# VectorE's order within a group of the RWKV stage: residual, bonus product and moments change places

## The chip, the core and the metric

The kernel runs on one core of one Trainium2 chip. The metric is device time in microseconds, the median of several runs. It has five engines that run side by side and meet through semaphores: TensorE (PE; its weight loads are shown apart as PEld), VectorE (DVE), ScalarE (ACT), GpSimd (POOL) and SyncE (SP), which issues transfers here. Each takes its instructions in the order of its own program. On-chip memory is SBUF, and PSUM in banks, where PE writes.

## What is computed

The kernel is a chain of eight residual stages over x of shape 32 x 256 x 128 in float32. The change touches the first alone, an RWKV time mix behind a layernorm:

```python
shifted = jnp.pad(x, ((0, 0), (1, 0), (0, 0)))[:, :T]
delta = shifted - x
low = jnp.tanh((x + delta * mu_x) @ W_x1).reshape(B, T, 5, PROJ_LR)
mus = jnp.einsum('blnr,dnr->blnd', low, W_x2) + x_bias
xr, xw, xk, xv, xg = [x + delta * mus[:, :, i] for i in range(5)]
...
def step(S, inp):
    o_t = einsum('bhk,bhkv->bhv', r_t, S) + einsum('bhk,hk,bhk,bhv->bhv', r_t, u, k_t, v_t)
    S = exp(w_t)[..., None] * S + k_t[..., :, None] * v_t[..., None, :]
...
o = (o - mean) * rsqrt(var + EPS)          # per head
o = (o * gn_w + gn_b) * (g * sigmoid(g))
return o @ W_o                             # added to x
```

## The kernel before

`stage_rwkv` (from L282) works on 8192 tokens as 16 groups (NG) of 512 tokens, two sequences each. Its loop on every engine is a software pipeline written out by hand: one pass g holds work for group g-2 (end) up to group g+3 (start), and the order inside a pass is the order in which the engine does it. A step starts once the semaphores named in it are up.

VectorE's steps, by group p:

- `moments` (L359): mean and variance of the input rows, four bn_stats (L366) and seven small operations, the last of them vareps (L380).
- `mix_in` (L382): xm, the input of the low-rank projection. `mix_out` (L388), five times: xi from PE's mixes in PSUM.
- `outer` (L394), four times: kv, PE's value times key. The third value on PE waits for the first kv, the fourth for the second.
- `scan` (L401), four times two scans (L407) over 256 steps: the recurrence. Its inputs are dec and kv, both in SBUF.
- `bonus_key` (L410): ruk. `bonus_value` (L416): cv, PE's product c, in PSUM bank 3, times vv.
- `gate` (L422): gg from th (ScalarE) and PE's gate product.
- `variance` (L428) and `normalise` (L432): per-head norm, in n.
- `gated` (L450): z = nt * gg. `residual` (L456): PE's y, in PSUM bank 4, added to x.

GpSimd does `inverse` (L503): rstd and shift from vareps and the mean, `difference` (delta), three `add_x` (L519) and four `read` (L526) a pass. ScalarE's pass (L762) runs: square of group g-1, evac g+2, tw, vv, root (L691: logarithm and exponential of the norm), key, decay, gate (th, L735), receptance (rr), then `layernorm(g+3)` (four xn, L748, which wait for shift), then `affine(g-1)` (nt, L718), then the two low-rank tanh (L760). PE's pass (L658) runs: four values (L556), five mixes (L568), out g-2 (L633), heads g-1 (L643, L647), turn_in g+2 (L575, which writes bank 4 and waits for residual g-2), then decay_low, plain_value, key, decay, gate, bonus (L618), receptance, turn_back g-1 (L592), low_rank g+2 (L654, L656). The first low-rank product writes bank 3, so it waits for cv:

```python
def low_rank(p):
    pe.wait_ge(s["xm_done"], p + 1)
    at_least(pe, s["cv_done"], p - 1)
```

Of the kernel before, what the change touches and what calls it, by code (L numbers as in the profile page):

```python
# [84 lines left out]
def at_least(eng, sem, v):  # L85

    if not (isinstance(v, int) and v <= 0):
        eng.wait_ge(sem, v)
# [193 lines left out]
def stage_rwkv(nc, k, tag, w, x_in, arrive, loads):  # L282
# [5 lines left out]
    with ExitStack() as ctx:  # L288
# [54 lines left out]
        has = lambda p: 0 <= p < NG  # L343
# [8 lines left out]
        def _(dve):  # L352
# [29 lines left out]
            def mix_in(p):  # L382
                dve.wait_ge(s["delta_done"], p + 1)
                at_least(dve, s["low_done"], 2 * p)
                nc.vector.scalar_tensor_tensor(out=seq(xm[:]), in0=seq(delta[:, p % 2, :]), scalar=w["a_mux"][:, 0:1], in1=x(p),
                                               op0=ALU.mult, op1=ALU.add).then_inc(s["xm_done"], 1)

            def mix_out(p, j):  # L388
                i = ORDER[j]
                dve.wait_ge(s["mus_done"], 5 * p + j + 1)  # L390
                nc.vector.scalar_tensor_tensor(out=xi[:, i, :], in0=at[f"m{j}"], scalar=w["a_xb"][:, i:i + 1],
                                               in1=delta[:, p % 2, :], op0=ALU.add, op1=ALU.mult).then_inc(s["dm_done"], 1)

            def outer(p, v):  # L394
                dve.wait_ge(s["v_done"], VQ * p + v + 1)
                if v == 0:
                    dve.wait_ge(s["k_out"], p + 1)
                at_least(dve, s["scan_done"], VD * (p - 1) + 2 * v + 2)
                nc.vector.tensor_tensor(kv[:, v, :], vp[:, v % 2, :], kk[:, p % 2, :], ALU.mult).then_inc(s["kv_done"], 1)

            def scan(p, v):  # L401
                if v == 0:
                    dve.wait_ge(s["dec_done"], p + 1)
                dve.wait_ge(s["kv_done"], VQ * p + v + 1)
                at_least(dve, s["rs_done"], VQ * (p - 1) + v + 1)
                for b in range(2):
                    nc.vector.tensor_tensor_scan(S[:, v, b, 1:T + 1], dec[:, p % 2, b * T:(b + 1) * T], kv[:, v, b * T:(b + 1) * T], 0.0,  # L407
                                                 ALU.mult, ALU.add).then_inc(s["scan_done"], 1)

            def bonus_key(p):  # L410
                dve.wait_ge(s["r_out"], p + 1)
                at_least(dve, s["c_done"], p)
                nc.vector.scalar_tensor_tensor(out=ruk[:], in0=rr[0:HK, p % 2, :], scalar=w["a_u"][0:HK, 0:1], in1=kk[0:HK, p % 2, :],
                                               op0=ALU.mult, op1=ALU.mult).then_inc(s["ruk_done"], 1)

            def bonus_value(p):  # L416
                dve.wait_ge(s["c_done"], p + 1)
                dve.wait_ge(s["vv_out"], p + 1)
                at_least(dve, s["oc_done"], p)
                nc.vector.tensor_tensor(cv[:], at["c"], vv[:, p % 2, :], ALU.mult).then_inc(s["cv_done"], 1)  # L420

            def gate(p):  # L422
                dve.wait_ge(s["th_done"], p + 1)
                at_least(dve, s["z_done"], p - 2)
                nc.vector.scalar_tensor_tensor(out=gg[:, p % 3, :], in0=th[:], scalar=1.0, in1=at["gate"],
                                               op0=ALU.add, op1=ALU.mult).then_inc(s["gg_done"], 1)

            def variance(p):  # L428
                dve.wait_ge(s["sq_done"], p + 1)
                nc.vector.tensor_reduce(out=ss[:], in_=sq[:], axis=AX.X, op=ALU.add).then_inc(s["norm"], 1)  # L430

            def normalise(p):  # L432
                base = NORM * p
                dve.wait_ge(s["norm"], base + 1)
                nc.vector.tensor_scalar(ve[:], ss[:], 1.0 / VD, LN_EPS, ALU.mult, ALU.add).then_inc(s["norm"], 1)
                dve.wait_ge(s["y0_done"], p + 1)
                dve.wait_ge(s["norm"], base + 2)
                nc.vector.tensor_tensor(nw[:, 0, :], ve[:], y0[:], ALU.mult).then_inc(s["norm"], 1)
                dve.wait_ge(s["norm"], base + 3)
                nc.vector.scalar_tensor_tensor(out=nw[:, 1, :], in0=nw[:, 0, :], scalar=-0.5, in1=y0[:],  # L440
                                               op0=ALU.mult, op1=ALU.mult).then_inc(s["norm"], 1)
                dve.wait_ge(s["norm"], base + 4)
                nc.vector.scalar_tensor_tensor(out=nw[:, 2, :], in0=nw[:, 1, :], scalar=1.5, in1=y0[:],
                                               op0=ALU.add, op1=ALU.mult).then_inc(s["norm"], 1)
                dve.wait_ge(s["norm"], base + 5)
                at_least(dve, s["nT_done"], p)
                nc.vector.tensor_tensor(heads_of(n[:]), heads_of(oc[:]), nw[:, 2, :][:, :, None].to_broadcast([P, GT * HA, VD]),
                                        ALU.mult).then_inc(s["n_done"], 1)

            def gated(p):  # L450
                dve.wait_ge(s["nt_out"], p + 1)
                dve.wait_ge(s["gg_done"], p + 1)
                at_least(dve, s["y_done"], p)
                nc.vector.tensor_tensor(z[:], nt[:], gg[:, p % 3, :], ALU.mult).then_inc(s["z_done"], 1)

            def residual(p):  # L456
                dve.wait_ge(s["y_done"], p + 1)
                xg = k.X[:, p * GT:(p + 1) * GT, :].rearrange("p a b -> p (a b)")
                nc.vector.tensor_tensor(xg, at["y"], xg, ALU.add).then_inc(s["res_done"], 1)

            for g in range(-3, NG + 2):
                if has(g - 2):
                    gated(g - 2)
                if has(g):
                    for v in range(VQ):
                        outer(g, v)
                if has(g + 1):
                    mix_out(g + 1, 0)
                    mix_out(g + 1, 1)
                if has(g):  # L470
                    scan(g, 0)
                    bonus_key(g)
                if has(g + 1):
                    mix_out(g + 1, 2)
                    mix_out(g + 1, 3)
                    mix_out(g + 1, 4)
                if has(g):
                    scan(g, 1)
                if has(g - 2):
                    residual(g - 2)  # L480
                if has(g):
                    scan(g, 2)
                    scan(g, 3)
                if has(g - 1):
                    variance(g - 1)
                if has(g + 2):
                    mix_in(g + 2)
                if has(g - 1):
                    normalise(g - 1)
                if has(g + 3):  # L490
                    moments(g + 3)
                if has(g + 1):
                    gate(g + 1)
                if has(g):
                    bonus_value(g)
            dve.wait_ge(s["res_done"], NG)

        @block.gpsimd
# [2293 lines left out]
```

## Time and profile before

| | |
|---|---|
| Time, median of 3 runs | 3493.65 us (3492.93 to 3501.08) |
| The profiled execution | 3497.12 us, its span 3495.3 us |
| RWKV stage | from 16.2 to about 490 us of the span |
| PE busy over the whole span | 3058.7 us (88%) |
| DVE | 2353.5 us (67%) |
| ACT | 1738.7 us (50%) |
| POOL | 1241.1 us (36%) |
| VectorE's 128 scans in this stage, mean | 1163 ns |

The rows are read so. A timeline row gives start, length, engine, line, operation, what is written and read, the number of instructions merged, and in brackets how long the engine stood idle before it and who ended that. A windows row gives a stretch, its length, the busy time of each engine in it, and the granted TensorE clock (PEclk, 1.00 being full) in that stretch. On VectorE the next instruction starts up to 0.08 us before the profile has the one before it end.

### The profile page before, as it was taken

The numbers are of one execution on the slowest core, as the hardware profiler recorded it, in microseconds if no ns is written. First come the engines' busy times: TensorE is split into PE (matmuls) and PEld (weight loads), VectorE is DVE, ScalarE is ACT, GpSimd is POOL, SyncE is SP. The second block draws the span as 40 slices with busy tenths as digits, with TensorE's granted clock in tenths as the row PEclk, the third lists the DMA queues.
The fourth block names the chain that finished last, engine by engine and source line by source line (L and its number), as shares of the span: only waits on it lengthen the run. The fifth ranks groups of instructions, "written<-read, shape, count | busy, mean of one in ns | idle before, by whom it ended". The sixth has DMA issues, their size and how long they took to land. (4 is left out here: it accounts for less than half of the span.)

```text
span 3495.3 us, 49585 instructions
## 1 busy us (share of the span) xinstructions
PE 3058.7 (88%) x16500; PEld 2031.7 (58%) x16500; DVE 2353.5 (67%) x5412; ACT 1738.7 (50%) x3804; POOL 1241.1 (36%) x1238
## 2 busy tenths in 40 slices
PE   6999974999883799999649998889799999999989
PEld 2555554888741344444548887679645555555557
DVE  4888876555465677776655555213489999999964
ACT  2444321333352699999313333225366666666644
POOL 3444431000023477777310000422134444444432
PEclk9999976999997799999769999559999999999999
DMA  3000012111032101000221100000000000000001
GB/s 113 1 1 1 1 31 76 37 37 35 1 104 92 41 26 30 28 27 16 83 71 37 37 29 27 0 0 1 1 1 1 1 1 1 1 1 1 1 13 37
DMA packets 106556, 91.30 MB, mean 26 GB/s; under 512 B 15373, under 2 KB 96147, under 8 KB 104000
## 3 DMA queue, kind: packets, MB, share of 16 engines
q1 hardware_dynamic: 104928, 87.31, 7.9%
q8 instruction: 135, 2.21, 0.3%
q14 instruction: 117, 0.96, 0.1%
q10 hardware_dynamic: 1376, 0.82, 0.1%
HBM read 57.66 MB, written 30.15 MB: 25 GB/s over the span
## 5 line engine op out<-in xcount | busy, mean ns | idle before, releaser
L2370 ACT ACTIVATE m_x_hT<-m_x_hid,wm_b 128x260 f32<-128x260 f32 x512 | 242.8, 478 | 437.1 <-PE m_x_hid L2292 437.1
L1319 POOL TENSOR_TENSOR c_tE<-c_tE,c_tDm 128x256 f32<-128x256 f32 x512 | 373.4, 730 | 138.8 <-ACT c_tE L1279 125.4
L1202 DVE TENSOR_REDUCE c_tM<-c_tpa 128x2 f32<-128x512 f32 x512 | 330.2, 682 | 131.3 <-PE c_tpa L1104 130.4
L1279 ACT ACTIVATE c_tE<-c_tpb 128x512 f32<-128x512 f32 x512 | 310.0, 607 | 43.2 <-PE c_tpb L1121 43.2
L2292 PE MATMUL m_x_hid<-m_x_xg,wm_w 128*128 128x260 f32 x1024 | 306.7, 386 | 8.8 <-ACT m_x_hT L2370 5.3
L2300 PE MATMUL m_x_yp<-m_x_hT,wm_w 128*128 128x260 f32 x1024 | 301.1, 384 | 0.0
L1655 POOL TENSOR_TENSOR b_wkv<-b_at,b_rec 128x512 f32<-128x512 f32 x128 | 163.3, 1276 | 305.9 <-DVE b_rec L1591 305.9
L2148 POOL TENSOR_TENSOR rstd_all<-m_x_vareps,m_x_neg_half 128x8 f32<-128x8 f32 x16 | 26.4, 1649 | 654.0 <-DVE m_x_vareps L2231 654.0
L1104 PE MATMUL c_tpa<-c_tK,c_Qm 96*128 96x256 f16 x1024 | 205.3, 283 | 49.8 <-DMA c_Qm<-aug_d 36.6
L1121 PE MATMUL c_tpb<-c_Qm,c_tK 101*128 101x256 f16 x1024 | 198.8, 276 | 23.5 <-ACT c_tE L1279 23.4
L1260 ACT ACTIVATE c_tDm<-wc_pos,c_LD 128x128 f32<-128x128 f32 x512 | 209.0, 411 | 20.7 <-PEq L96 20.7
L2300 PEld LDWEIGHTS m_x_yp<-m_x_hT,wm_w 128*128 128x128 f32 x1024 | 194.3, 191 | 29.6
L1649 POOL TENSOR_TENSOR b_dt<-b_er,b_bt 128x512 f32<-128x512 f32 x128 | 163.6, 1278 | 129.9 <-DVE b_er L1575 96.7
L2186 DVE TENSOR_SCALAR m_x_yT<-m_x_yp,wm_b 128x260 f32<-128x260 f32 x128 | 62.6, 489 | 216.6 <-PE m_x_yp L2300 216.6
L2292 PEld LDWEIGHTS m_x_hid<-m_x_xg,wm_w 128*128 128x128 f32 x1024 | 183.2, 191 | 42.5 <-ACT m_x_hT L2370 15.8
L1104 PEld LDWEIGHTS c_tpa<-c_tK,c_Qm 96*128 96x128 f16 x1024 | 70.7, 98 | 168.5 <-DVE c_tM L1202 88.8
L2333 PE MATMUL m_x_misc<-m_x_ys,m_x_sel 104*128 104x128 f32 x1280 | 151.9, 276 | 4.2 <-DVE m_x_ys L2201 4.2
L2532 PE MATMUL r_rec<-r_ring,wr_a 128*128 128x32 f32 x512 | 128.5, 340 | 29.5 <-ACT r_ring L2609 29.5
L2333 PEld LDWEIGHTS m_x_misc<-m_x_ys,m_x_sel 104*128 104x128 f32 x1280 | 146.6, 192 | 7.7 <-DVE m_x_ys L2201 7.7
L1748 PE MATMUL b_y<-b_wos,b_gts 128*128 128x128 f32 x1024 | 148.6, 288 | 0.0
L407 DVE TENSOR_TENSOR_SCAN a_S<-a_dec,a_kv 128x256 f32<-128x256 f32 x128 | 142.7, 1163 | 0.0
L82 POOL TENSOR_TENSOR rstd<-vareps,neg_half 128x4 f32<-128x4 f32 x48 | 54.1, 1127 | 248.4 <-DVE vareps L71 248.4
(345 smaller groups left out, 7388.2 us busy)
## 6 DMA issues: line engine op xcount, KB each, us to landing
m_x_ir<-idx_d SPq DMA_DIRECT2D x16, 1040.0 KB, 6.6
xn_d<-xn SPq DMA_DIRECT2D x32, 256.0 KB, 2.3
m_x_xs<-xn_d SPq DMA_DIRECT2D x16, 512.0 KB, 4.1
c_tK<-k_d SPq DMA_DIRECT2D x32, 192.0 KB
c_Qm<-q_d SPq DMA_DIRECT2D x128, 48.0 KB
wm_w<-in_m_w SPq DMA_DIRECT2D x2, 2048.0 KB, 10.4
gate_d<-c_pgate SPq DMA_DIRECT2D x16, 256.0 KB
q_d<-c_phi SPq DMA_DIRECT2D x32, 128.0 KB
```

The source lines that it names most:

```text
L1104: m = nc.tensor.matmul(pa[:, h % 2, qt, :], lhsT=Qm[0:QROWS, u, h, qt * P:(qt + 1) * P], rhs=K[0:QROWS, u, h // HG, :], start=True, stop=T ...
L1121: m = nc.tensor.matmul(pb[:, h % 2, kt * T:(kt + 1) * T], lhsT=K[:, u, h // HG, kt * P:(kt + 1) * P], rhs=Qm[:, u, h, :], start=True, stop ...
L1202: nc.vector.tensor_reduce(out=M[:, u % 2, 2 * h:2 * h + 2], in_=pa[:, h % 2], axis=AX.X, op=ALU.max).then_inc(s["max_done"], 1)
L1260: nc.scalar.activation(Dm[:, u % 2, h, :], w["c_pos"][:], ACT.Exp, scale=LD[:, bass.ds(b * HB + h, 1)]).then_inc(s["dexp"], 1)
L1279: nc.scalar.activation(E[:, h % 8].rearrange("p a q -> p (a q)"), pb[:, h % 2, :], ACT.Exp).then_inc(s["exp_done"], 1)
L1319: nc.gpsimd.tensor_tensor(diag, diag, Dm[:, u % 2, h:h + 1, :].to_broadcast([P, 2, P]), ALU.mult).then_inc(s["dmul_done"], 1)
L1649: nc.gpsimd.tensor_tensor(dt_[:, m % 2, :], er[:, m % 4, :], bt[:, m % 2, :], ALU.add).then_inc(s["d_done"], 1)
L1655: nc.gpsimd.tensor_tensor(wkv[:, m % 2, :], at_[:, m % 4, :], rec[:, m % 2, :], ALU.mult).then_inc(s["wkv_done"], 1)
L2292: nc.tensor.matmul(hid[:, c % 2, 0:QW], lhsT=w["m_w1"][:, e, j * P:(j + 1) * P], rhs=xg[:, slot, e, :, :].rearrange("p b c -> p (b c)"), s ...
L2300: mm = nc.tensor.matmul(yp[:, e % 2, 0:QW], lhsT=w["m_w2"][:, e, j, :], rhs=hT[:, e % 2, j, :], start=(j == 0), stop=(j == NJH - 1))
L2333: mm = nc.tensor.matmul(misc[:, bank, h * D:(h + 1) * D], lhsT=sel[:, b, c, h * P:(h + 1) * P], rhs=ys[:, b % 2, c, :], start=(c == 0), st ...
L2370: nc.scalar.activation(hT[:, e % 2, j, :], hid[:, c % 2, 0:QW], ACT.Gelu, bias=w["m_b1"][:, c:c + 1]).then_inc(s["gelu_done"], 1)
```

## The change

Only VectorE's loop is edited, and only the order. In a pass, residual of group g-2 comes ahead of the second scan of group g and no longer behind it. Behind normalise the order was moments(g+3), gate(g+1), bonus_value(g); it becomes bonus_value(g), gate(g+1), moments(g+3).

```diff
                     mix_out(g + 1, 4)
-                if has(g):
-                    scan(g, 1)
                 if has(g - 2):
                     residual(g - 2)
                 if has(g):
+                    scan(g, 1)
                     scan(g, 2)
                     scan(g, 3)
...
                 if has(g - 1):
                     normalise(g - 1)
+                if has(g):
+                    bonus_value(g)
+                if has(g + 1):
+                    gate(g + 1)
                 if has(g + 3):
                     moments(g + 3)
-                if has(g + 1):
-                    gate(g + 1)
-                if has(g):
-                    bonus_value(g)
```

## Rows read from the trace of the kernel before

**Rows 1.** Busy time by stretch: an odd pass and an even one, variance to variance.
```profile
core 0: us, PE busy (x) PEld busy (x) DVE busy (x) ACT busy (x) POOL busy (x), PEclk, DMA share, GB/s
231.21:258.22 27.01, 25.24 (x101) 14.01 (x100) 22.91 (x41) 11.69 (x21) 12.28 (x11) 1.00 0.00 1
258.22:285.77 27.55, 25.24 (x101) 14.01 (x100) 23.45 (x41) 11.70 (x21) 12.82 (x11) 1.00 0.00 1
```

**Rows 2.** Waits, 0 to 420 us: who waited for whom, us in total, times, longest.
```profile
DVE a_z L454 <- ACT a_nt L718: 30.7, 12, 2.6
...
PE a_bank L654 <- DVE a_cv L420: 21.4, 13, 5.9
```

**Rows 3.** Timeline of VectorE, end of pass 7 and start of pass 8.
```profile
258.22 0.65 DVE L430 TENSOR_REDUCE a_ss<-a_sq 128x64 f32<-128x512 f32 x1
...
262.32 0.86 DVE L366 BATCH_NORM_STATS2 stats<-X 128x6 f32<-128x128 f32 x4
...
263.84 0.17 DVE L380 TENSOR_SCALAR a_vareps<-dev 128x4 f32<-128x4 f32 x1
263.92 0.69 DVE L425 SCALAR_TENSOR_TENSOR a_gg<-a_th,a_bank 128x512 f32<-128x512 f32 x1
264.53 0.68 DVE L420 TENSOR_TENSOR a_cv<-a_bank,a_vv 128x512 f32<-128x512 f32 x1
267.77 0.69 DVE L454 TENSOR_TENSOR a_z<-a_nt,a_gg 128x512 f32<-128x512 f32 x1 [2.56 <-ACT a_nt L718]
```

**Rows 4.** Timeline of GpSimd, same pass.
```profile
264.09 1.02 POOL L507 TENSOR_TENSOR a_rstd<-a_vareps,neg_half 128x4 f32<-128x4 f32 x1 [3.91 <-DVE a_vareps L380]
```

**Rows 5.** Timeline of ScalarE, same pass.
```profile
258.91 0.35 ACT L694 ACTIVATE a_lnv<-a_ss,a_epsc 128x64 f32<-128x64 f32 x1
...
262.58 0.60 ACT L735 ACTIVATE a_th<-a_bank 128x512 f32<-128x512 f32 x1
...
265.43 1.65 ACT L748 ACTIVATE xn<-X,a_shift,a_rstd 128x128 f32<-128x128 f32 x4 [1.10 <-POOL a_shift L509]
266.98 0.76 ACT L718 ACTIVATE a_nt<-a_bank,a_gw 128x512 f32<-128x512 f32 x1
```

**Rows 6.** Timeline of PE, pass 7: its two waits for VectorE.
```profile
254.21 0.63 PE L575 MATMUL a_bank<-ident,xn 128*128 128x128 f32 x4 [0.47 <-DVE X L459]
...
265.36 1.10 PE L654 MATMUL a_bank<-a_xm,wa_wx 128*128 128x512 f32 x2 [1.21 <-DVE a_cv L420]
```

**Rows 7.** Timelines of VectorE and GpSimd, narrow stretches of pass 7, single scans.
```profile
251.43 1.47 DVE L407 TENSOR_TENSOR_SCAN a_S<-a_dec,a_kv 128x256 f32<-128x256 f32 x1
...
250.93 1.43 POOL L519 TENSOR_TENSOR a_xi<-a_xi,a_xT 128x512 f32<-128x512 f32 x1 [0.26 <-DVE a_xi L391]
...
253.41 0.66 DVE L459 TENSOR_TENSOR X<-a_bank,X 128x512 f32<-128x512 f32 x1
...
256.02 0.66 DVE L407 TENSOR_TENSOR_SCAN a_S<-a_dec,a_kv 128x256 f32<-128x256 f32 x1
```

**Rows 8.** Timelines of PE and VectorE behind pass 0, and in passes 13 and 14.
```profile
71.26 2.05 PE L654 MATMUL a_bank<-a_xm,wa_wx 128*128 128x512 f32 x2 [5.92 <-DVE a_cv L420]
...
76.76 0.69 DVE L399 TENSOR_TENSOR a_kv<-a_vp,a_kk 128x512 f32<-128x512 f32 x1 [5.64 <-PE a_vp L556]
...
426.87 0.69 DVE L425 SCALAR_TENSOR_TENSOR a_gg<-a_th,a_bank 128x512 f32<-128x512 f32 x1 [0.80 <-ACT a_th L735]
...
453.52 0.69 DVE L425 SCALAR_TENSOR_TENSOR a_gg<-a_th,a_bank 128x512 f32<-128x512 f32 x1 [2.12 <-ACT a_th L735]
```

**Rows 9.** Busy time and clock by stretch: pauses of PE and what followed.
```profile
98.03:100.16 2.13, 0.00 (x0) 0.02 (x1) 1.94 (x9) 0.45 (x1) 1.16 (x2) 1.00 0.00 0
100.70:103.90 3.20, 3.20 (x5) 1.33 (x4) 0.69 (x1) 2.67 (x7) 0.00 (x0) 0.50 0.00 0
...
597.84:603.80 5.96, 3.45 (x18) 2.94 (x19) 1.39 (x4) 3.23 (x6) 2.13 (x1) 1.00 0.02 10
3353.87:3360.20 6.33, 2.77 (x13) 2.69 (x14) 3.80 (x4) 2.00 (x4) 4.15 (x3) 0.74 0.00 0
```

## The prediction

> **What bounds the kernel now.** Only the RWKV stage is touched, the first 490 us of the span. I read it by group: one pass of VectorE's loop. The table by stretch, cut from one variance (L430) to the next, gives 27.01 us for an odd pass and 27.55 for an even one [rows 1]. PE is busy 25.2 of them, VectorE 22.9 and 23.5. So no engine is full, and the question is which ring of waits sets 27.01. The waits of the stage name two candidates [rows 2]: VectorE's product z waits for nt 12 times, 30.7 us, and PE waits for VectorE's cv 13 times, 21.4 us. The timelines of one pass tell them apart. VectorE ends the moments (L366 to L380) at 264.01, does gate and cv, then sits idle 2.56 us in front of z at 267.77 [rows 3]. That idle time is a ring: rstd on GpSimd starts 0.08 after vareps ends and has waited 3.91 for it [rows 4]; ScalarE's xn waits 1.10 for shift and starts at 265.43, and nt stands behind the four xn in ScalarE's queue, 266.98 to 267.74; z starts 0.03 later [rows 3, 5]. From z on VectorE is busy but for short waits up to the next moments. So **the ring is VectorE from z to vareps, then GpSimd, ScalarE, z**: 23.25 us (240.76 to 264.01) + 3.76 us. PE follows it: its pause of 1.21 in front of L654 (it waits for cv), 0.47 in front of L575 (it waits for residual) [rows 6], and some 0.25 inside the values, whose third matmul needs the first kv, which stands right behind z, are slack: 27.01 - 1.93 = 25.1 us is PE's own work.
>
> **Part 1, the moments go last.** Nothing is added or removed: every instruction of the pass is there in both orders, no DMA is moved and SyncE is not touched. What changes is what stands in front of what. Before, vareps was ready 1.69 us after normalise had been issued (262.32 to 264.01). Now cv (0.61 from start to start) and gate (0.61) stand ahead of it, and gate also has to wait for th: cv would be done with its slot at 262.93, th ends at 263.18 [rows 3, 5], so gate starts at 263.21, 0.28 later. vareps is late by 0.61 + 0.61 + 0.28 = 1.50 us. Behind it on the ring are rstd, shift, xn, nt and z, with no slack in any of them, so z is late by **1.50**; queued behind z are the four kv and with them PE's third value. The idle 2.56 in front of z becomes 3.9: the two products that once filled part of this wait are now in front of it. Bounds: without the wait for th 1.22; if nothing else gives, 1.50. I take 1.50.
>
> **Part 2, cv comes early.** PE's 1.21 pause in front of L654 goes. PE does the low-rank pair and two values earlier, then waits for the first kv. Off the ring: worth 0 in a full pass, and 1.2 if PE were the bound.
>
> **Part 3, residual ahead of the second scan.** PE's 0.47 goes too (1.0 in even passes), also off the ring. But there is a second effect, on VectorE itself. A scan has two SBUF inputs, and takes 0.66 alone (256.02) but 1.47 when it starts beside GpSimd's add (251.43) [rows 7]; it ends 0.54 after the add does (250.93 + 1.43 = 252.36, and 252.90). The scan seems to stand still until GpSimd is done. The residual, with one input in PSUM, took 0.66 whatever ran. Put in front of the scan, it fills 251.43 to 252.01, and the scan still ends at 252.90: 0.58 saved. GpSimd's next read then starts just behind a scan instead of just behind a residual, as at 256.02, and is held for the scan's end, about 0.18 later than now. Net **-0.40**, from variance on, and th moves with it, since the logarithm (L694, 258.91) starts 0.04 after variance ends and the ring's ScalarE part is busy from there [rows 5]. Bounds: 0 (the residual is slowed as a scan is) to -0.58.
>
> **A full pass:** 1.50 - 0.40 = **+1.10 us**, for the 11 passes g = 2 to 12. Group 1's pass differs: there kv already waits for PE, since L654 starts late there; the delay of z falls into that wait and nets -0.2.
>
> **The head and the tail.** In pass 0 PE stands 5.92 us in front of L654 for cv and VectorE then 5.64 for PE [rows 8]. cv comes about 2.2 us earlier (it was behind moments and gate), and PE leaves half clock a little sooner: -2.5. In passes 13 to 15 there are no moments. In 13 (gate's wait is 0.80, at 426.87 [rows 8]) PE sets the pace and loses its waits of about 0.5 for cv and 0.5 for residual: -1.0. In 14 gate waits 2.12 for th [rows 8], which hangs on variance: -0.4, and -0.4 in 15. Together -1.8. **Order alone: 12.1 - 0.2 - 2.5 - 1.8 = +7.6 us.**
>
> **The clock.** PE's slack is now in one piece. 28.1 - 25.1 = 3.0 us of idle between second and third value in odd passes, 28.65 - 25.1 = 3.5 in even ones. The trace of before has the case: in pass 1 PE idled 2.15 us (98.03 to 100.16) at full clock, 2.4 GHz, and the next 3.2 us ran at 0.50, 1.2 GHz [rows 9]. Pauses of 1.21 in the passes after it did nothing: both passes of [rows 1] stand at 1.00. In the whole span I count 9 pauses of 2.4 to 3.7 us out of full clock, the first at 597.8, which left the clock up, the last at 3353.9, which did not [rows 9]; 7 of the 9 were followed by half clock. The half-clock stretch was 3.4 us in five of the seven and 6.8 in two. What runs in it here is the third and fourth value and the first two mixes, some 3.7 us of work at full clock, and VectorE waits for each: all on the ring. Cost of a drop: half of 3.4 = 1.7, up to some 3.0 for the long one; mean 2.1. Over the 12 passes with moments: 12 x 7/9 x 2.1 = **+19 us** (bounds: 0, and 12 x 3.0 = 36).
>
> The Trainium skill (TensorE: Matmul & The Clock Gate, "Why this matters for your kernels") puts the pause that sends the clock to half rate above the one that I work out for the odd passes. By that page the order alone would be left in those, and at most the even ones would pay: some +7.6 to +18. The row of 2.15 us speaks against it, and the measurement decides.
>
> **Sum.** 7.6 + 19 = +26.6. The profiled execution took 3497.1 us, 3.5 above the median 3493.65, its span being 3495.3. The differences are worked out within that execution and are carried to the median: 3493.65 + 26.6 = **3520**.
>
> **Rivals.**
> 1. The clock stays up (the page's rule, or pauses that fall kindly): only the order counts, +7.6, **3501**. For it: two of nine pauses. Against it: seven, and 2.15 in this very stage.
> 2. PE is the bound after all: both of its waits go in 12 passes, 12 x 1.68 = 20 less, **3473**. For it: PE is the busiest engine, 25.2 of 27.0 [rows 1]. Against it: the idle time in front of z, closed without slack from vareps on [rows 3 to 5]. It would decide if kv did not stand behind z. This is the case on the other side.
> 3. The edit does next to nothing: the later vareps is absorbed (ScalarE not held by shift), and residual's 0.40 in 14 passes stays, -6: **3488**. Against it: xn's wait of 1.10 is already positive.
> 4. The long half-clock stretch every time, since even passes leave a rest of the pause behind the drop: 7.6 + 12 x 3.0 = +44, **3537**.
>
> **How the numbers follow.** The forecast (order and clock together, its own range 3510 to 3531) 0.62; rival 1 0.16; rival 2 0.07; rival 3 0.05; rival 4 0.10. The range 3500 to 3533 leaves out rivals 2 and 3 and most of 4: some 0.2. About 0.3%, or 10.5 us, is what a measurement can tell from no change: faster is rival 2 with a little of 3, 0.08; within it rival 1 and the rest of 3, 0.20; slower 0.72.
>
> **What the profile of the changed kernel would show.** z's idle time about 3.9 in passes 1 to 12 instead of 2.56, with nt as its releaser, and the moments ending some 1.1 later against variance. No wait of L654 for cv and none of L575 for residual. One pause of PE of about 3 us in front of the third value, put down to kv. The second scan's first half 0.9 long instead of 1.47. And PEclk in the slices of the stage below full, with kv and the first mixes of VectorE waiting for PE. The forecast fails if the clock stays full through the stage (then rival 1), or if z does not move against variance (rival 3), or if kv no longer follows z (rival 2).

## The result and the profile after

The changed kernel took **3530.61 us** (median of 7 runs, 3513.46 to 3540.64) against 3501.08 us (median of 7, 3492.93 to 3511.01) for the kernel before: a ratio of 1.0081, 95% interval 1.0064 to 1.0097. It is slower by 0.8%, 22 to 34 us. The profiled execution has a span of 3528.8 us against 3495.3. Nearly all of the 33.5 us between the spans, 33.2, lies in the RWKV stage: its last instruction on VectorE (the last residual) ends at 523.00 instead of 489.78, and what follows takes 3005.8 us instead of 3005.5.

Beside [rows 3] belongs one more row of the kernel before, that of n (L447):

```profile
261.72 0.69 DVE L447 TENSOR_TENSOR a_n<-a_oc,a_nw 128x512 f32<-128x512 f32 x1
```

The changed kernel's timeline of VectorE, from the end of pass 7 (an odd one) into pass 8:

```profile
276.29 0.69 DVE L447 TENSOR_TENSOR a_n<-a_oc,a_nw 128x512 f32<-128x512 f32 x1
276.89 0.68 DVE L420 TENSOR_TENSOR a_cv<-a_bank,a_vv 128x512 f32<-128x512 f32 x1
277.72 0.69 DVE L425 SCALAR_TENSOR_TENSOR a_gg<-a_th,a_bank 128x512 f32<-128x512 f32 x1
279.84 0.17 DVE L380 TENSOR_SCALAR a_vareps<-dev 128x4 f32<-128x4 f32 x1
283.76 0.69 DVE L454 TENSOR_TENSOR a_z<-a_nt,a_gg 128x512 f32<-128x512 f32 x1 [3.75 <-ACT a_nt L717]
284.37 1.28 DVE L399 TENSOR_TENSOR a_kv<-a_vp,a_kk 128x512 f32<-128x512 f32 x2
287.22 0.69 DVE L399 TENSOR_TENSOR a_kv<-a_vp,a_kk 128x512 f32<-128x512 f32 x1 [1.57 <-PE a_vp L555]
288.93 0.69 DVE L399 TENSOR_TENSOR a_kv<-a_vp,a_kk 128x512 f32<-128x512 f32 x1 [1.01 <-PE a_vp L555]
290.64 0.75 DVE L391 SCALAR_TENSOR_TENSOR a_xi<-a_bank,wa_xb,a_delta 128x512 f32<-128x512 f32 x1 [1.02 <-PE a_bank L567]
291.79 0.75 DVE L391 SCALAR_TENSOR_TENSOR a_xi<-a_bank,wa_xb,a_delta 128x512 f32<-128x512 f32 x1 [0.40 <-PE a_bank L567]
```

cv now stands right behind n, and vareps starts 3.55 behind n where it started 2.12 behind it (263.84 against 261.72). z's idle time is 3.75 instead of 2.56, still ended by nt. New are the waits of kv and of the first mixes for PE: 1.57, 1.01, 1.02 and 0.40, where the passes before had 0.53, 0.17, 0.17 and 0.11. PE's timeline of the same pass, and its pauses with the clock (windows: stretch, length, busy times, PEclk), answer to [rows 6, 9]:

```profile
278.56 1.02 PE L653 MATMUL a_bank<-a_xm,wa_wx 128*128 128x512 f32 x2
...
280.28 1.88 PE L555 MATMUL a_vp<-a_xi,wa_wv 128*128 128x512 f32 x4
285.11 3.78 PE L555 MATMUL a_vp<-a_xi,wa_wv 128*128 128x512 f32 x4 [2.95 <-DVE a_kv L399]
```

```profile
101.35:437.98 336.63, 303.83 (x1100) 164.98 (x1100) 233.14 (x441) 127.25 (x221) 139.19 (x110) 0.89 0.00 1
251.43:253.50 2.07, 0.00 (x0) 0.00 (x0) 0.42 (x1) 2.07 (x6) 0.00 (x0) 1.00 0.00 0
253.55:260.30 6.75, 5.87 (x7) 2.52 (x8) 3.15 (x6) 0.46 (x1) 0.00 (x0) 0.50 0.00 0
282.16:284.20 2.04, 0.00 (x0) 0.00 (x0) 0.44 (x1) 2.04 (x6) 0.00 (x0) 1.00 0.00 0
284.30:291.00 6.70, 5.89 (x7) 2.52 (x8) 3.10 (x6) 0.39 (x1) 0.00 (x0) 0.50 0.00 0
```

L653 (L654 of before) no longer waits for cv. PE's slack is one pause in front of the third value, and it comes out of it at half clock (1.2 GHz): the four matmul records of two values take 3.78, against 1.98 in a pass of e3 (below) that stays at full clock. The drop comes while PE still stands: the stretch from 253.55 is at 0.50, though PE's busy time in it is 5.87 of 6.75. Over the 11 passes from the first kv of pass 2 to that of pass 13 the mean clock is 0.89.

From here on a pass is measured from its first kv to the next pass's first kv, and its mean is taken over these 11 (before: 104.72 to 405.02, 27.30 each; after: 101.35 to 437.98, 30.60).

### The profile page after: what moved, and what is told of

The parts are those of the page before. It is cut to its first block and busy times, and to the rows that moved or that the text cites. A ratio compares the mean times of both kernels' runs of the same rounds, so it can differ in the third digit from the quotient of the medians.

```text
span 3528.8 us, 49585 instructions
## 1 busy us (share of the span) xinstructions
PE 3087.4 (87%) x16500; PEld 2042.6 (58%) x16500; DVE 2326.5 (66%) x5412; ACT 1735.7 (49%) x3804; POOL 1239.5 (35%) x1238
## 5 line engine op out<-in xcount | busy, mean ns | idle before, releaser
L1747 PEld LDWEIGHTS b_y<-b_wos,b_gts 128*128 128x128 f32 x1024 | 124.8, 192 | 27.9 <-issue 27.9
## 6 DMA issues: line engine op xcount, KB each, us to landing
wm_w<-in_m_w SPq DMA_DIRECT2D x2, 2048.0 KB, 10.6
```

The source lines that it names most:

```text
L1747: mm = nc.tensor.matmul(y[:, b * 2 + h, :], lhsT=gts[:, m % 2, c, :], rhs=wos[:, cc * GT + c, :], start=(m == 0 and c == 0), stop=(cc == N ...
```

## The experiments

All are edits in `stage_rwkv`. The ratios are to runs of the kernel before on the same chip.

| kernel | pass, us | stage ends | time, median | ratio, 95% interval |
|---|---|---|---|---|
| before | 27.30 | 489.78 | | |
| changed | 30.60 | 523.00 | 3530.61 | 1.0081 (1.0064 to 1.0097) |
| e9, changed again | 30.62 | 522.43 | 3531.64 | 1.0084 (1.0053 to 1.0114) |
| e1, residual alone | 26.60 | 480.84 | 3491.04 | 0.9965 (0.9949 to 0.9980) |
| e7, e1 + cv ahead of gate | 26.60 | 474.33 | 3489.09 | 0.9963 (0.9949 to 0.9977) |
| e2, end of the pass alone | 30.19 | 518.26 | 3532.35 | 1.0097 (1.0065 to 1.0128) |
| e3, changed, pause filled | 27.96 | 495.87 | 3505.35 | 1.0019 (1.0006 to 1.0033) |
| e5, changed, half filled | 28.52 | 500.12 | 3515.81 | 1.0039 (1.0024 to 1.0054) |
| e6, before, nt ahead of xn | 27.14 | 487.94 | 3501.39 | 0.9993 (0.9979 to 1.0007) |
| e10, before, xn last | 27.13 | 487.87 | 3503.38 | 1.0005 (0.9991 to 1.0020) |
| e4, changed, nt ahead of xn | 25.65 | 464.80 | 3472.26 | 0.9922 (0.9901 to 0.9944) |
| e8, changed, xn last | 24.73 | 448.80 | 3459.52 | 0.9892 (0.9869 to 0.9916) |

### The two edits apart: e1 and e2

e1 moves residual alone:

```diff
-                if has(g):
-                    scan(g, 1)
                 if has(g - 2):
                     residual(g - 2)
                 if has(g):
+                    scan(g, 1)
                     scan(g, 2)
```

> The kernel before with residual ahead of the second scan, the end of the pass left as it was (moments, gate, bonus product). Theory (the ring z, moments, rstd, xn, nt, z sets the pass, and residual is hidden behind GpSimd's add): passes shorter by 0.4 in odd and 0.9 in even ones, the stage ends some 9 us before 489.8, ratio 0.997 to 0.998, z's idle time stays 2.56 and the clock full after pass 2. Rival 1 (PE's turn_in waiting for residual is what counts): 0.47 and 1.0 a pass, about the same sum, but then z's idle time must shrink. Rival 2 (off the path): stage within 1 us.

Measured: passes 26.60, which is 0.40 less in odd passes (27.00 before) and 0.95 less in even ones (27.55 before), 0.70 on the mean; the stage is 8.9 us shorter, z's idle time 2.56 as before. The total came out as expected and rival 1, which wanted less idle time in front of z, did not; nor did rival 2. How the gain comes about is in two timelines of e1, VectorE and then GpSimd, in an odd pass:

```profile
247.44 0.67 DVE L459 TENSOR_TENSOR X<-a_bank,X 128x512 f32<-128x512 f32 x1
248.03 3.58 DVE L407 TENSOR_TENSOR_SCAN a_S<-a_dec,a_kv 128x256 f32<-128x256 f32 x6
251.54 0.65 DVE L430 TENSOR_REDUCE a_ss<-a_sq 128x64 f32<-128x512 f32 x1
254.76 1.56 DVE L385 SCALAR_TENSOR_TENSOR a_xm<-a_delta,wa_mux,a_xT 128x512 f32<-128x512 f32 x1 [2.56 <-POOL a_delta L513]
```

```profile
246.93 1.09 POOL L518 TENSOR_TENSOR a_xi<-a_xi,a_xT 128x512 f32<-128x512 f32 x1 [0.27 <-DVE a_xi L391]
...
249.37 4.36 POOL L525 TENSOR_TENSOR a_rS<-a_S,a_rr 128x512 f32<-128x512 f32 x2 [1.35 <-DVE a_S L407]
253.69 1.03 POOL L513 TENSOR_TENSOR a_delta<-a_xT 128x512 f32<-128x512 f32 x1
254.69 1.08 POOL L525 TENSOR_TENSOR a_rS<-a_S,a_rr 128x512 f32<-128x512 f32 x1
```

With residual, which has an input in PSUM, in its shadow, GpSimd's add takes 1.09 instead of 1.43 [rows 7] and is over at 248.02, just as the first scan starts. So that scan is not held at all. The six scans then run without a gap, 0.58 apart, and now it is GpSimd that stands: its first two reads take 4.36. The price comes later, 2.56 in front of xm for delta, so the variance is early and the pass gains less than the scans do: in odd passes variance starts 2.68 earlier against the first kv, xm only 0.41. These 0.41 are the shorter delta, which starts where it did and takes 1.03 instead of 1.43. In even passes two scans are held for GpSimd's reads as before, only the one that stood for the add goes free, variance comes 0.94 earlier, and xm with it.

e2 is the other half, the kernel before with cv, gate, moments at the end of the pass:

```diff
                 if has(g - 1):
                     normalise(g - 1)
+                if has(g):
+                    bonus_value(g)
+                if has(g + 1):
+                    gate(g + 1)
                 if has(g + 3):
                     moments(g + 3)
-                if has(g + 1):
-                    gate(g + 1)
-                if has(g):
-                    bonus_value(g)
```

> The kernel before with the end of the pass alone changed (bonus product, gate, moments); residual stays behind the second scan. Theory: z late by 1.5 a pass, z's idle time about 3.75, PE's pause 2.5 to 3.5 us and half clock behind most of them; without residual's gain the stage is as long as with both edits or up to 8 us longer, unless the pauses fall more kindly: ends at 515 to 531, ratio 1.007 to 1.012. Rival (the two edits do harm only together, by moving PE's slack into one pause): PE's pause stays near 2, no half clock, stage ends at 489.8 + 12 x 1.5 = 508.

Measured: the stage ends at 518.26, z's idle time is 3.76 in passes 2 to 13, PE's pause 3.02 from pass 3 on. The end of the pass alone does the harm; the rival falls. Not every such pause brought half clock here, nine of the eleven from pass 3 to 13, each for 3.4 us. Windows of e2, a pause and what followed, twice:

```profile
189.74:192.74 3.00, 0.00 (x0) 0.00 (x0) 1.34 (x3) 2.59 (x6) 0.00 (x0) 1.00 0.01 3
192.80:196.20 3.40, 3.40 (x8) 1.57 (x9) 2.45 (x4) 0.00 (x0) 0.00 (x0) 1.00 0.01 2
218.23:221.23 3.00, 0.00 (x0) 0.00 (x0) 1.33 (x3) 2.60 (x6) 0.00 (x0) 1.00 0.00 0
221.90:225.10 3.20, 3.20 (x5) 1.24 (x4) 1.27 (x2) 0.00 (x0) 0.00 (x0) 0.50 0.00 0
```

Eight matmuls in 3.40 us behind the first pause, five in 3.20 behind the second; both pauses are 3.0 long. Half clock begins here only once PE is at work again, 0.2 to 1.4 us behind the end of the pause in all nine.

### Order and clock apart: e3 and e5

e3 gives PE something to do in the pause. What it adds is thrown away; heads overwrites the bank:

```diff
                     for v in range(VQ):
                         values(g, v)
+                        if v == 1 and has(g - 1):
+                            at_least(pe, s["n_done"], g - 1)
+                            for _ in range(2):
+                                nc.tensor.matmul(oc[:].rearrange("p a b -> p (a b)"), lhsT=w["a_wv"][:, v, :],
+                                                 rhs=xi[:, 3, :], start=True, stop=True, skip_group_check=True)
```

> The changed kernel with two more matmuls (128x512, some 0.86 us each) of a value product into the oc bank, which nothing reads then, between PE's second and third value: extra work that is thrown away and lies in the pause. Theory (3.0 us of a pass are half clock, started by that pause): the clock stays full in the stage, passes 27.7 to 28.4 instead of 30.7, stage ends at 488 to 497 instead of 523, some 30 us faster than the changed kernel although PE does more; ratio to the kernel before 0.999 to 1.003. Rival (PE is short of time anyway, half clock is only a sign of it): stage at 523 or later, ratio 1.008 or more.

Measured: passes 27.96, stage 495.87, ratio 1.0019. More work on PE made the stage 27 us shorter in the profile (495.87 against 523.00) and took the ratio from 1.0081 to 1.0019. The windows of e3, its 11 passes, and its PE in one pass:

```profile
103.25:410.77 307.52, 291.74 (x1144) 161.84 (x1144) 235.60 (x441) 127.32 (x221) 139.41 (x110) 1.00 0.00 1
```

```profile
240.40 1.88 PE L664 MATMUL a_oc<-a_xi,wa_wv 128*128 128x512 f32 x4
243.86 1.98 PE L555 MATMUL a_vp<-a_xi,wa_wv 128*128 128x512 f32 x4 [1.57 <-DVE a_kv L399]
```

There are 44 matmul records more (1144 against 1100), the pause is 1.57 or 1.28 from pass 3 on, the clock 1.00 throughout. Half clock was the cause of the long pass and not a sign of it. The order alone is what is left: 27.96 - 27.30 = 0.66 a pass (27.80 against 27.00 in odd passes, 28.09 against 27.55 in even ones). The filling itself adds nothing to it: in e5, with half of it, the passes at full clock are 27.8 and 28.1 long as well.

e5 is the same with `range(1)`.

> The changed kernel with one thrown-away 128x512 matmul between PE's second and third value instead of two. PE's pause should be 2.1 to 2.5 us a pass. Theory (a pause of that size in this stage can start half clock, as the one of 2.15 at 98 us did, but not each time): between no and ten stretches of half clock in passes 1 to 12, each costing 1.7 us or more, passes 28 to 30, stage ends between 496 and 517, ratio 1.002 to 1.008. Rival (only pauses near 3 us cost anything): passes 27.95 as with two matmuls, stage at 496.

Measured: pauses of 2.10 to 2.45 from pass 3 on; 3 of those 11 were followed by 3.4 us of half clock, and each such pass is 1.4 to 1.7 longer than its kind; so was the pause of 2.93 in pass 2. The four starts lie 85.3 apart, every third pass; passes 28.52 on the mean, stage 500.12. The rival falls: pauses well below 3 us cost something too. Windows of e5, a pause with it (2.44 long) and one without:

```profile
186.33:188.75 2.42, 0.00 (x0) 0.00 (x0) 1.33 (x3) 2.02 (x5) 0.00 (x0) 1.00 0.00 0
190.15:193.45 3.30, 3.30 (x5) 1.35 (x4) 1.57 (x3) 0.00 (x0) 0.00 (x0) 0.50 0.01 2
216.13:218.22 2.09, 0.00 (x0) 0.00 (x0) 1.34 (x3) 1.68 (x4) 0.00 (x0) 1.00 0.00 0
218.30:221.70 3.40, 3.40 (x8) 1.55 (x9) 2.45 (x4) 0.00 (x0) 0.00 (x0) 1.00 0.00 0
```

### Why every pass: e9

e9 is the changed kernel itself, executed again. In its first profile half clock had come in all 12 passes from 2 to 13, in the last 11 for 6.8 us, its starts 30.72 apart.

> The changed kernel as it is, executed and profiled once more. In its first profile a stretch of half clock of 6.8 us lay in each pass from 2 to 12, at distances of 30.72 us. Theory A (the pass settles at the length at which the stretch falls on the same place of each pass, whatever the start): the same again, passes 30.7 on the mean, stage ends at 521 to 525. Theory B (chance of one execution): stretches in 7 to 10 of 12 passes, some of 3.4 us, passes 29 to 30.5, stage at 505 to 520. Without any: 496.

Measured: the same, passes 30.62, stage 522.43, in 12 of 12 passes, 6.8 us in the last 11, starts 30.72 apart once more. Windows of e9, its 11 passes and two of the stretches:

```profile
100.64:437.42 336.78, 304.04 (x1100) 164.92 (x1100) 232.96 (x442) 127.32 (x221) 139.27 (x110) 0.89 0.00 1
130.20:136.80 6.60, 5.95 (x7) 2.52 (x8) 3.00 (x5) 0.23 (x1) 0.00 (x0) 0.50 0.00 0
160.90:167.50 6.60, 5.90 (x7) 2.52 (x8) 3.00 (x6) 0.28 (x1) 0.00 (x0) 0.50 0.00 0
```

Two executions settle at the same distance, so this is no chance of one. Whether they would from another start is open: the first stretch of half clock begins 1.98 behind the first kv of pass 2 in one and 2.11 in the other, nearly the same place. What makes them settle was not tried apart. e2, with nearly the same pause but without residual's move, did not settle: its passes run from 28.5 to 31.6. Its starts too are 30.72 apart in six of nine distances from pass 2 on, but two passes have none.

What the long stretches have in common is where they begin. All 22 of 6.8 us in the two executions begin 0.8 to 1.0 before the pause ends; the one long stretch of e2, in pass 2, begins 1.7 before the end of a pause of 3.78. The nine of e2 and the four of e5 that begin behind the pause last 3.4.

### Where cv counts: e7, e6, e10, e4 and e8

e7 is e1 with `moments`, `bonus_value`, `gate` at the end: the moments are not delayed, cv comes 0.6 earlier than in e1.

> Residual ahead of the second scan, moments first, then bonus product, then gate: moments are not delayed and cv comes 0.6 earlier than before. Theory (cv is off the ring): the same as with residual alone, passes 26.6, stage ends at 480 to 482, ratio 0.996 to 0.998, PE's pause cut in two pieces below 1.5 us each. Rival (PE's wait for cv is part of the path): 0.6 less a pass, passes 26.0, stage at 473.

Measured: passes 26.60, to the hundredth those of e1, so cv is off the path in full passes. The stage nevertheless ends 6.5 earlier than e1's, at 474.33. The first kv of pass 2 stands at 99.58 against 104.35, 4.8 earlier: 1.5 of it lie ahead of the first kv of pass 0, a point that moved by 0.7 between the two executions of the changed kernel as well, and 3.3 between there and pass 2, where PE waits for cv (5.33 and 1.60 against 5.91 and 2.15) and has one stretch of half clock of 3.4 us instead of one of 6.8 and one of 3.4. The other 1.7 lie in the tail. Head and tail were missed in the expectation.

The next four open the ring through ScalarE: nt goes ahead of the four xn in ScalarE's queue, so that z no longer waits for the moments. e4 (on the changed kernel) and e6 (on the one before):

```diff
+                if has(g - 1):
+                    affine(g - 1)
                 if has(g + 3):
                     layernorm(g + 3)
-                if has(g - 1):
-                    affine(g - 1)
                 if has(g + 2):
                     low_rank(g + 2, 0)
```

e8 and e10 put `layernorm(g + 3)` behind the two `low_rank` as well, on the changed kernel and on the one before.

> The changed kernel with ScalarE's affine (nt) ahead of its four xn, so that z no longer hangs on the moments. Theory (the ring through ScalarE's queue carries the late moments to z): z's idle time falls below 1 us, the pause in front of the third value goes, the clock stays full, and PE's own 25.1 us or VectorE set the pass at 25.5 to 26.5; stage ends at 465 to 478, ratio 0.993 to 0.997. Rival (z is late for another reason, n or PE's transposes of it): z's idle time stays above 3, stage above 510.

> The kernel before (moments, gate, bonus product; residual behind the second scan) with ScalarE's affine ahead of its four xn, to be held against the changed order with the same edit, whose passes take 25.6 us and whose stage ends at 464.8. Theory (with z off the moments' ring PE is the bound, and then its waits for cv and residual count): passes 26.3 to 27.0, stage ends at 472 to 483, so that the new order is worth 8 to 18 us here, against a loss of 33 with the ring. Rival (the new order is bad by itself): the stage ends at 465 or before.

e4: z's idle time is 0.00 in the full passes, passes 25.65, stage 464.80, as expected; the ring through moments, rstd, xn and nt is confirmed. e6 missed its expectation: z is free there too, and the pass is only 0.16 shorter. Its VectorE and its PE, one pass:

```profile
236.06 0.68 DVE L420 TENSOR_TENSOR a_cv<-a_bank,a_vv 128x512 f32<-128x512 f32 x1
236.66 0.68 DVE L454 TENSOR_TENSOR a_z<-a_nt,a_gg 128x512 f32<-128x512 f32 x1
239.75 0.69 DVE L399 TENSOR_TENSOR a_kv<-a_vp,a_kk 128x512 f32<-128x512 f32 x1 [2.40 <-PE a_vp L556]
```

```profile
236.89 1.10 PE L654 MATMUL a_bank<-a_xm,wa_wx 128*128 128x512 f32 x2 [1.21 <-DVE a_cv L420]
```

z follows cv at once, and now kv waits 2.40 for PE's first value, which stands behind the low-rank product, which waits for cv. This is **a second ring**: cv, L654, value, kv, mixes, scans, moments, cv. In the kernel before it is 0.16 a pass shorter than the first, and hides behind it. It is read from these waits; no run moves cv alone with the first ring open.

> The changed kernel with ScalarE's order affine, the two low-rank tanh, then the four xn. Theory: as with affine first (passes 25.6, stage at 464.8), and PE's remaining pause of 0.75 in front of the mixes, every other pass, goes because the tanh no longer stand behind xn: passes 25.2 to 25.4, stage ends at 461 to 464, ratio 0.991 to 0.993. Rival (PE is at its own work already): no change against 464.8; or xn of the later group come late and PE waits for them in turn_in: stage above 466.

> The kernel before with ScalarE's order affine, two low-rank tanh, four xn. Against the changed order with the same edit (passes 24.7, stage at 448.8). Theory (without the moments' ring a second ring, cv, low-rank product, values, kv, scans, cv, holds the order of before): tanh earlier changes nothing, passes 27.1 as with affine first, stage at 486 to 489, the new order then worth 38 us. Rival (PE at its own work sets it): passes below 26, stage below 475.

e10 is as e6 (27.13). e8 reaches 24.73, below its expectation of 25.2. In e4 PE's weight loads of the mixes had waited for the tanh; in e8 nothing is left. Waits of e4, 80 to 380 us, and windows of e8, its 11 passes:

```profile
PEld a_bank L567 <- ACT a_low L759: 16.3, 11, 2.0
```

```profile
94.38:366.41 272.03, 272.03 (x1101) 152.64 (x1100) 237.05 (x441) 130.06 (x220) 144.38 (x111) 1.00 0.00 1
```

PE is busy 272.03 of 272.03 us: the pass is PE's own work. The new order on VectorE, 33 us slower with the ring, is worth 39.1 us without it (487.87 of e10 against 448.80 of e8; how much of it is cv and how much residual was not tried apart), and e8 is faster than either kernel, 0.9892 of the one before.

## Why the prediction came out right

It forecast slower by 26.6 us for two reasons, the later moments on the ring and half clock behind PE's pause. Measured were 22 to 34 us by the ratio, 33.2 in the profiled stage. The predicted 3520 is 10.6 below the median of 3530.61; 7.4 of that is its anchor, the median of three runs, which became 3501.08 with seven. The mechanisms held in kind (later moments on the ring, one pause of PE, half clock behind it), and the sizes erred in both directions, so that the closeness of the total is in part luck. The readings on VectorE were made in pass 7, an odd one, and taken for all. Term by term, in the profiled executions:

- **vareps late by 1.50, z with it.** The row above says 1.43 (3.55 - 2.12). In time it cost 27.96 - 26.60 = 1.36 a pass (e3 against e1): 1.49 in even passes of e3, where gate waits 0.21 for th as forecast, and 1.20 in odd ones, where th is early with the variance and gate does not wait (the lower bound of the forecast was 1.22). Right.
- **residual -0.40.** In odd passes it was -0.40 to the hundredth, by another way; in even ones it was -0.95, so -0.70 on the mean (e1 against before), outside the bounds of 0 to -0.58. The step that failed is "the scan still ends at 252.90": it held GpSimd's add at its length, but the add had been slowed by the scan that stood behind it. Free of it, it ends 0.34 earlier, and the scan is not held (0.67, in even passes 0.72, where "0.9 long" was forecast). Nor does the gain run "from variance on" in odd passes: variance gained 2.68 there, and the pass only what delta gained. That the sum came out is luck.
- **A full pass +1.10**: it was +0.80 in odd passes and +0.54 in even ones, +0.66 on the mean.
- **cv early: 0.** Right for the full pass (e7). What the text did not see is the second ring, 0.16 behind, which would have spoilt any change that frees z alone (e6, e10).
- **Head -2.7, with the -0.2 of pass 1.** The first kv of pass 2 came 104.72 - 101.35 = 3.4 earlier; 0.6 of this lies ahead of the first kv of pass 0 (49.03 and 48.45), within what two executions of one kernel differ by there. The rest is 2.8: right.
- **Tail -1.8.** The passes from 14 on gained 1.3; pass 13 lies in the clock's term. e7, in which pass 13 runs at full clock, went from 84.76 to 82.16 behind the first kv of pass 13, -2.6.
- **Clock +19.** Between the first kv of pass 2 and of pass 14 the changed kernel takes 364.29 us and e3 332.25: 32.0 us, 2.7 a pass, within the bounds but near their end of 36. Two factors failed: 7 of 9 was 12 of 12, and the mean cost of 2.1 was that of a mix with short stretches, where 11 of 12 were the long ones. The step behind it took the passes for independent draws. The pause of 3.5 that it gave the even passes was not there either: all from pass 3 on were 2.95 to 3.04 long.
- **Sum.** Order -3.4 + 5.8 - 1.3 = +1.2 (from unrounded terms) where 7.6 was forecast, clock 32.0 where 19 was: 33.2 and 26.6. The order was put 6.4 too high and the clock 13 too low, so that the first error took back half of the second. (5.8 is e3 against before from pass 2 to 14, 332.25 - 326.43.)

Rival 4, the long stretch every time, is the rival that the clock bore out, against the forecast's own term: 11 of 12 were long, since the drop came 0.8 to 1.0 before the pause was over, in odd passes as in even ones. Its +44 was too high mostly because the order cost 1.2 and not 7.6, and because a stretch cost 2.7 and not 3.0. So the forecast's +26.6 is nearer to the 33.2, but with the rival's clock and not with its own.

Rival 1, the clock that stays up, fell: it is what e3 shows when the pause is filled, 0.2% slower than before, and not what the changed kernel does. The Trainium skill (TensorE: Matmul & The Clock Gate, "Why this matters for your kernels") warns of pauses of TensorE above about 3 us. The measurement decides otherwise here, at that length and below it: of the pauses of 2.9 to 3.1 us from pass 3 on, all 22 in the two executions of the changed kernel and 9 of 11 in e2 ended in half clock, and of those of 2.1 to 2.5 in e5 3 of 11.

Rival 2, PE as the bound, was wrong for this kernel, and right for the kernel with the ring opened: there the order on VectorE pays more than the rival's 20 us, 39.1.

Rival 3, the later vareps absorbed, fell with z: it came 1.20 and 1.49 later in e3, and z's idle time is 3.75.

## What to carry to other kernels

Behind the instruction that an engine waits at, look for the work that ends the wait: idle time in front of z was not room for cv and gate, since the moments that released z came behind them on the same engine. When a change gathers an engine's small pauses into one, price the clock too, for every pass and not by chance, because a loop can bring the drop at the same place of each pass; where it falls while the engine still stands, take the long stretch. And read both kinds of pass when a loop alternates: what held in the odd pass here did not hold in the even one. And look for the ring behind the ring: VectorE's order and ScalarE's order each opened one, and only both edits together (e8) let PE run without a pause.

## What the runs showed of the hardware

- Work that does nothing can save time. Two discarded matmuls a pass, 1.88 us of PE, made the stage 27 us shorter (e3).
- Half clock came at a steady distance of 30.72 us, 11 times in a row, in both executions of the changed kernel. In e2, with a pause of 3.02, it left out two passes of eleven; in e5, with 2.10 to 2.45, it came every third pass.
- The half clock was long (6.8 us) where it began 0.8 to 1.7 us before PE's pause ended, and short (3.4 us) where it began behind it, in all passes from 2 to 13 of the two executions of the changed kernel, e2 and e5. In pass 0 of e7 it began 0.5 before the end of a pause of 5.33, and was short.
- VectorE's scans with two SBUF inputs and GpSimd's operations hold each other, and who starts first does not settle alone which one stands. In odd passes of e1 GpSimd's read, started 0.16 behind a scan, stood through three more scans (two reads took 4.36 us); in even passes the same read, started 0.15 behind a scan, took 1.39 and the next scan stood, 1.51. What decides between the two is open. The Trainium skill (SBUF — State Buffer, "SBUF: two separate sides") says that whoever starts first has the shared port for the whole instruction and the other blocks; the even passes agree, and the odd ones go further, since a waiting GpSimd operation can be passed over by one scan after another. The even pass in e1, VectorE and then GpSimd:

```profile
276.22 2.09 DVE L407 TENSOR_TENSOR_SCAN a_S<-a_dec,a_kv 128x256 f32<-128x256 f32 x2
```

```profile
276.37 1.39 POOL L525 TENSOR_TENSOR a_rS<-a_S,a_rr 128x512 f32<-128x512 f32 x1 [1.21 <-DVE a_S L407]
```
